# Normalised rows of two layers moved from ScalarE to VectorE, and the expert slots, routing and softplus steps of a two-layer kernel put in another order

## The reference

```python
# layer 0, mixer: 16 heads of 64
Q = x @ W_Q + b_Q; K = x @ W_K + b_K; V = x @ W_V + b_V
x = x + softmax(Q K^T / 8) V @ W_O + b_O            # x on the right is layernorm(x)
# layer 0, feed-forward: top-1 of 8 experts, 512 hidden
gates = softmax((x @ wg_red.T) @ unit(wg).T); e = argmax(gates)
x = x + max(gates) * (gelu(x @ w1[e] + b1[e]) @ w2[e] + b2[e])
# layer 1, mixer: a Mamba block, 256 channels, 16 states
h = x @ fc1.T + b;  xc, z = split(h @ in_proj.T)
u = silu(causal_conv4(xc) + conv_b);  dt_low, Bm, Cm = split(u @ x_proj.T)
dt = softplus(dt_low @ dt_proj.T + dt_b)
state = exp(dt * A) * state + (dt * u) * Bm;  y = sum(state * Cm) + u * D
x = x + (y * silu(z)) @ out_proj.T @ fc2.T + fc2_b
# layer 1, feed-forward: every one of 8 experts (256 hidden), summed, times a gate close to 1
```

## Time and profile before

| | us |
|---|---|
| median of 3 runs | 1217.61 |
| the profiled execution | 1217.61 |
| its span, first to last instruction | 1216.3 |
| PE busy | 1128.7 (93%) |
| DVE busy | 832.1 (68%) |
| POOL busy | 781.9 (64%) |
| ACT busy | 583.4 (48%) |

### The profile page before, as it was taken

The page is one execution under the profiler, slowest core; times in us unless marked ns, Lnnn a source line. Parts: engine busy times, 40 slices in busy tenths (PEclk is TensorE's granted clock), DMA queues, the critical chain, the costliest instruction groups (busy, mean ns, idle before and its releaser), DMA issues.

```text
span 1216.3 us, 19302 instructions
## 1 busy us (share of the span) xinstructions
PE 1128.7 (93%) x7541; PEld 660.3 (54%) x7541; DVE 832.1 (68%) x1248; ACT 583.4 (48%) x805; POOL 781.9 (64%) x410
## 2 busy tenths in 40 slices
PE   5899999999999999999999999968788988779998
PEld 2455555555555555555655556956434434335786
DVE  5565567566566566556575556535889889998887
ACT  3434444443443444443434444537864576443654
POOL 4577778677777777767579882272586678883100
PEclk9899999999999999999999999989898989999999
DMA  6000000000000000000000115364463344440000
GB/s 195 2 1 1 1 1 1 2 1 1 2 2 1 2 1 1 2 2 1 1 2 14 51 48 195 100 199 187 157 216 132 118 136 138 147 147 18 9 9 18
DMA packets 38058, 68.83 MB, mean 57 GB/s; under 512 B 5936, under 2 KB 24112, under 8 KB 37968
## 3 DMA queue, kind: packets, MB, share of 16 engines
q1 hardware_dynamic: 32624, 47.75, 12.3%
q0 software_dynamic: 5344, 19.86, 4.7%
HBM read 61.30 MB, written 6.16 MB: 55 GB/s over the span
## 4 chain that ended last, share of the span: by engine, by line
PE 77%; DVE 8%; issue 6%; POOL 6%; ACT 3%; DMA 1%; POOLq 0%; SPq 0%; DVEq 0%; ACTq 0%
PE psum L564 19%; PE psum L533 16%; PE psum L550 6%; PE psum L580 5%; PE psum L537 5%; POOL hc L1937 4%; PE psum L642 3%; PE psum L926 3%; PE psum L845 3%; PE psum L909 3%; PE psum L595 2%; PE psum L615 2%; DVE psum L1632 2%; PE psum L708 2%; DVE hs L1639 2%
## 5 line engine op out<-in xcount | busy, mean ns | idle before, releaser
L1830 POOL TENSOR_TENSOR psums<-psums,prob 128x1024 f32<-128x1024 f32 x180 | 426.6, 2370 | 104.2 <-ACT prob L998 82.7
L1347 DVE TENSOR_REDUCE mx<-psum 128x2 f32<-128x1024 f32 x256 | 302.0, 1220 | 211.2 <-PE psum L550 211.2
L998 ACT ACTIVATE prob<-psum 128x1024 f32<-128x1024 f32 x256 | 243.1, 1025 | 218.2 <-PE psum L537 218.2
L564 PE MATMUL psum<-prob,V 128*64 128x512 f32 x1024 | 258.4, 604 | 0.0
L1937 POOL TENSOR_TENSOR hc<-hs,cc 128x1024 f32<-128x1024 f32 x64 | 151.3, 2364 | 73.9 <-DVE hs L1639 72.7
L1639 DVE TENSOR_TENSOR_SCAN hs<-dA,psum 128x1024 f32<-128x1024 f32 x64 | 146.3, 2287 | 2.7 <-DVE psum L1632 0.7
L845 PE MATMUL psum<-hc,ident 128*128 128x512 f32 x256 | 126.7, 619 | 3.0 <-POOL hc L1937 2.9
L564 PEld LDWEIGHTS psum<-prob,V 128*64 128x64 f32 x1024 | 62.0, 136 | 98.3 <-issue 92.6
L1830 POOL TENSOR_TENSOR psums<-prob 128x1024 f32<-128x1024 f32 x30 | 71.5, 2382 | 62.9 <-ACT prob L998 62.9
L533 PE MATMUL psum<-q_hi,k_hi 64*128 64x512 f32 x512 | 108.4, 419 | 0.0
L537 PE MATMUL psum<-guard,row_one 64*128 64x512 f32 x512 | 101.7, 393 | 2.2 <-DMA guard<-mrow 2.2
(11 more groups left out here) (255 smaller groups left out, 1702.6 us busy)
## 6 DMA issues: line engine op xcount, KB each, us to landing
cc<-C_rows SPq DMA_DIRECT2D x64, 512.0 KB, 3.7
slots_in<-e_zero SPq DMA_DIRECT2D x2, 960.0 KB, 8.2
slots_out<-e_y SPq DMA_DIRECT2D x30, 64.0 KB, 3.1
slot_rows_h<-slots_in SPq DMA_DIRECT2D x6, 256.0 KB, 3.0
x<-in_x SPq DMA_DIRECT2D x2, 512.0 KB, 5.1
e_w<-in_e_w SPq DMA_DIRECT2D x1, 1024.0 KB, 8.8
out_x<-x SPq DMA_DIRECT2D x4, 256.0 KB, 2.3
wk<-in_wk SPq DMA_DIRECT2D x1, 512.0 KB, 4.7
```

Source lines behind the costliest of these rows:

```text
L564: ins = pe.matmul(A.O[HALF[s], :], A.V[pair % 2][:, j, s * DH:(s + 1) * DH], A.prob[unit(pair, c, j) % NPB][:, s * CH:(s + 1) * CH], start ...
L998: act.activation(A.prob[n % NPB][:, :], slots.bank("score", pair, c, j).rearrange("p s n -> p (s n)"), ACT.Exp, scale=float(DH) ** -0.5).t ...
L1347: dve.tensor_reduce(K.A.mx[:, :, t, c], slots.bank("max", pair, t, c), AXX, ALU.max).then_inc(*slots.inc("max", pair, t, c))
L1830: pool.tensor_tensor(total[:, :], (K.A.prob[(n - 1) % NPB] if j == 1 else total)[:, :], K.A.prob[n % NPB][:, :], ALU.add).then_inc(*K.psum ...
```

## The change

No arithmetic changes. `ACT_ROWS` loses 1 and 2, so the rows of the norms in pair 3 and pair 9 are normalised on DVE, and POOL no longer forms `shift` for them. In the expert slots of batch 0, `total` and `count` stand one to two slots later, and batch 1's first three weight fetches no longer stand ahead of the scatters. Batch 1's first slots stand later: before, three `up` and two `down` come ahead of the norm of the Mamba block, now two `up` and one `down`. In the first inputs the slots are interleaved with the taps in another way, the last two `up` and `gelu` stand ahead of `xpj`, and `xpj` waits for both halves of `u`. In the recurrence `yrow` of slots s+11 to s+14 stand one unit earlier, `back` and `rescale` too, `readd` of the second half one later, and the softplus steps of batch 1 are drawn together.

```diff
-ACT_ROWS, XDR_UNIT = (1, 2, 5, 6), 26
+ACT_ROWS, XDR_UNIT = (5, 6), 26
...
-                        6: [("logits", 1), ("choose", 1)], 7: [("total", 1), ("count", 1, 0), ("count", 1, 1)] + [("fetch", NSLOT + i) for i in range(3)],
-                        8: [("count", 1, 2)] + [("scatter", 1, q) for q in range(4)]}
+                        6: [("logits", 1), ("choose", 1)], 8: [("total", 1), ("count", 1, 0)], 9: [("count", 1, 1)],
+                        10: [("count", 1, 2)] + [("scatter", 1, q) for q in range(4)]}
...
-        beside[t // 2 + 6] += [("back", 1, t)]
-        beside[t // 2 + 8 + t // 6] += [("rescale", t)]
+        beside[t // 2 + 5] += [("back", 1, t)]
+        beside[t // 2 + 7 + t // 6] += [("rescale", t)]
...
-           2: [("down", n), ("down", n + 1), ("up", n + 2), ("up", n + 3), ("rate", 1), ("du", 0, 1)],
-           3: [("yrow", n), ("yrow", n + 1), ("gelu", n + 2), ("gelu", n + 3)], 4: [("down", n + 2), ("down", n + 3)],
+           2: [("down", n), ("down", n + 1), ("yrow", n), ("yrow", n + 1), ("up", n + 2), ("up", n + 3), ("rate", 1), ("du", 0, 1)],
+           3: [("gelu", n + 2), ("gelu", n + 3)], 4: [("down", n + 2), ("down", n + 3), ("yrow", n + 2), ("yrow", n + 3), ("e1_load",)], 6: [("wturn",)],
...
-           27: [("dtp", 1, 0), ("dtp_out", 1, 0)], 28: [("softexp", 1, 0)], 29: [("softlog", 1, 0), ("dt", 1, 0)], 30: [("du", 1, 0)], 31: [("inp", 1, 2)], 32: [("inp_out", 1, 2)],
+           27: [("dtp", 1, 0), ("dtp_out", 1, 0), ("softexp", 1, 0), ("softlog", 1, 0)], 28: [("dt", 1, 0)], 29: [("du", 1, 0)], 31: [("inp", 1, 2)], 32: [("inp_out", 1, 2)],
...
-        for k in range(KI):
-            pe.wait_ge(X.u_done, k + 1)
-            for c in range(NC):
...
+        pe.wait_ge(X.u_done, KI)
```

More of the change, by code:

```diff
@@ L272, in routed_order @@
         order += beside.get(n, []) + [("loads", n - 2)] * (n < 12) + [("skip",)] * (n == NSLOT)
-    order += [("rows", 1, 0), ("rows", 1, 1)] + [("back", 0, t) for t in range(NT)] + [("fetch", s + 3), ("fetch", s + 4)]
+    order += [("rows", 1, 0), ("rows", 1, 1)] + [("back", 0, t) for t in range(NT)] + [("fetch", s), ("fetch", s + 1)]
     order += [("turn", 1, 0), ("turned", 1, 0), ("rows", 1, 2), ("turn", 1, 1), ("turned", 1, 1), ("rows", 1, 3)]
-    order += [("up", s), ("gelu", s), ("up", s + 1), ("gelu", s + 1), ("down", s), ("down", s + 1)]
@@ L276, in routed_order @@
-    order += [("turn", 1, 2), ("turned", 1, 2), ("turn", 1, 3), ("turned", 1, 3), ("up", s + 2), ("gelu", s + 2)]
-    order += [("return", 0, t) for t in range(NT)] + [("lnvar", 4), ("lnroot", 4)] + [("fetch", s + i) for i in range(5, 13)]
-    return order + [("yrow", s), ("yrow", s + 1), ("lnrows", 4)]
+    order += [("return", 0, t) for t in range(NT)] + [("lnvar", 4), ("lnroot", 4)] + [("fetch", s + i) for i in range(2, 10)]
+    order += [("turn", 1, 2), ("turned", 1, 2), ("turn", 1, 3), ("turned", 1, 3), ("up", s), ("gelu", s), ("lnrows", 4)]
@@ L281, in first_inputs_order @@
+    return order + [("up", s + 1), ("gelu", s + 1), ("down", s), ("yrow", s)]
 def first_inputs_order():
     s = NSLOT
[L285 to L293, removed]
+    order = turned(4) + [("up", s + 2), ("fc1", 0), ("fc1_out", 0), ("gelu", s + 2), ("down", s + 1)]
@@ new lines, in first_inputs_order @@
+    order += [("inp", 0, 0), ("inp_out", 0, 0), ("yrow", s + 1), ("up", s + 3), ("gelu", s + 3), ("inp", 0, 1), ("inp_out", 0, 1), ("down", s + 2)]
+    taps = [("conv", 0, k, w) for k in range(KI) for w in range(DCONV)]
+    order += [taps[0], ("yrow", s + 2), taps[1], *slot(s + 4), ("fetch", s + 10)]
+    for i in range(1, 4):
+        order += taps[2 * i:2 * i + 2] + slot(s + 4 + i) + [("fetch", s + 10 + i)]
+    order += [("fetch", s + 14), ("up", s + 8), ("gelu", s + 8), ("down", s + 7), ("yrow", s + 7), ("silu", 0, 0), ("silu", 0, 1)]
@@ L294, in first_inputs_order @@
+    order += [("up", s + 9), ("down", s + 8), ("yrow", s + 8), ("gelu", s + 9), ("up", s + 10), ("gelu", s + 10), ("xpj", 0), ("xpj_take", 0), ("pick",), ("xpj_out", 0), ("dtp", 0, 0), ("xdr", 0), ("dtp", 0, 1)]
+    order += [("down", s + 9), ("yrow", s + 9), ("dtp_out", 0, 0), ("dtp_max",), ("softexp", 0, 0), ("down", s + 10), ("yrow", s + 10)]
     return order + [("softlog", 0, 0), ("dtp_out", 0, 1), ("dt", 0, 0), ("du", 0, 0)]
@@ L781, in pe_xpj @@
     if b == 0:
-        for k in range(KI):
-            pe.wait_ge(X.u_done, k + 1)
-            for c in range(NC):
[L785 to L791, removed]
+        pe.wait_ge(X.u_done, KI)
     for c in range(NC):
-        pe.wait_ge(*work.empty("mix", KI - 1, c))
+        if b:
+            pe.wait_ge(*work.empty("mix", KI - 1, c))
         pe.wait_ge(*work.free("xpj", b, c))
```

7 lines of the change are left out of this document (3 added, 4 removed).

## The result

| | before | after |
|---|---|---|
| median of 4 runs, us | 1217.39 (1215.68 to 1217.79) | 1228.59 (1227.26 to 1232.72) |
| ratio | | 1.0100, 95% interval 1.0074 to 1.0128 |
| profiled execution, its span | 1217.61, 1216.3 | 1229.24, 1227.9 |

Slower by 11.2 us; the two profiled executions differ by 11.6. The forecast was 1234.0 with a range of 1219 to 1238: the direction is right, the measured time lies inside the range, and the size is 5.4 us too high.

A forecast was written before the change was run, and what follows sets the result against it. PE was taken to bound attention, a chain of small steps and transfers 800 to 825 us, DVE the recurrence. 13.8 + 2.8 + 3.0 - 4.8 + 2.7 - 1.1 = +16.4 on 1217.6 gave 1234.0 us, range 1219 to 1238.

The forecast's parts named there:

- The norms: Attention, pairs 3 and 9: DVE's rows wait behind POOL's adds and make PE 6.9 us late in each pair, +13.8 us.
- each add (2.4 us) stands between two DVE rows: Norms in attention: POOL is let in after one DVE row, so DVE is done only at 212.9.
- rival 2: Norms: two rows pass between two adds, 2.6 us less per norm, +11.2 in all, 1228.8 us; chance 0.13.
- the forecast's 6.9: PE's lateness in us per norm pair, from waits for the `max` product's slot and then the output product's slot.
- Rival 1: Norms: the rows pass without waiting for further adds, only +2.6 is left, 1220.2 us; chance 0.26.
- Expert slots and the way to `fc1`: Scatters 0.8 us earlier, but `fc1` later behind slots waiting for weights; between +1.5 and +5.1, taken as +2.8 us.
- To the end of SiLU: First inputs: DVE stands 2.3 us before the second tap, and `gelu` of s+8 ahead of SiLU adds 0.7: +3.0 us.
- SiLU to unit 0: First inputs: Abs starts 5.1 us after SiLU instead of 10.0, first unit at 13.85 us instead of 18.7: -4.8 us.
- Recurrence: `yrow` ahead of units 3 and 5 costs +1.4 and +0.9, `readd` after unit 12 another 0.4: +2.7 us.
- Softplus of batch 1: Recurrence: unit 30's scan 2.2 us late, but `du` for unit 32 there 2.2 us earlier: -1.1 us.
- its 2.6 for the orders: All terms outside the norms, what is left if the rows pass: +2.6 us.

The follow-up runs named there:

- rows: The kernel before with only the norm rows of pairs 3 and 9 moved to DVE, every order as before: 1231.14 us, ratio 1.0104.
- split44: rows with four of the eight norm rows left in place and four moved behind the copy of `mrow`: 1239.17 us, ratio 1.0002.
- order: The changed kernel with the norm rows of pairs 3 and 9 back on ACT, so only the order changes: 1218.51 us, ratio 1.0001.
- tail: The kernel before with the last two `up` and `gelu` of batch 1 ahead of `xpj`: 1219.68 us, ratio 1.0001.
- swap: order with the second tap ahead of the `yrow` of s+2: 1244.75 us, one run.
- best: tail with the changed kernel's order of the recurrence: 1220.77 us, ratio 1.0008.
- tail2: tail with `up` and `gelu` of s+8, `down` and `yrow` of s+7 also ahead of the SiLU: 1235.35 us, ratio 0.9960.
- best2: tail2 with the changed kernel's order of the recurrence: 1236.42 us, ratio 0.9975.
- split56: rows with five norm rows first in pair 3 and six in pair 9, the rest later: 1243.73 us, one run.
- split77: rows with seven norm rows first in both pairs and one later: 1240.37 us, one run.

## Why the prediction was right, and where not

**The norms: mechanism right, size wrong (+13.8, measured +9.3).** DVE's rows stood behind POOL's adds in pairs 3 and 9, five passed first, and PE waited for the slot of the first `max` product. What failed is "each add (2.4 us) stands between two DVE rows". Two rows pass between adds: POOL's next add begins 0.15 us after the last has ended, and in that time the waiting row gets in and the next one right behind it. DVE was done at 211.2 - 1.7 = 209.5 instead of 212.9, with two adds in the way instead of three. The row on which 0.14 us of POOL's delay was read the earlier trace rows concerned DMA issues, not adds, and couldn't carry "one row, one add".

That is rival 2 (0.13), whose +4.3 a norm stands against 4.65 in each pair. The nearness is partly luck. Its 4.3 is all wait; the trace has 2.84 and 2.88 us of wait, and most of the other 1.8 is that PE's next steps ran at 1.2 GHz, a price that only the upper end of the forecast's range had. The wait for the output product, the last part of the forecast's 6.9, isn't there in after (in rows it is 0.37 us in pair 3 and 0.21 in pair 9). Rival 2's time, 1228.8, was met by luck too: the profile of after has 3.3 us in attention that no term had (the late start, the clock near 600 us), and the orders took back 1.3 where rival 2 had +2.6. Rival 1 ("the rows pass") is what split44 makes true, not the change.

The Trainium skill ("SBUF — State Buffer", "SBUF: two separate sides") has the lock held for a whole instruction by whoever comes first. The trace agrees, by the rows of 2.55 and 2.45 us that end as an add ends. What happens between two adds the rows show: two short DVE operations pass.

**Expert slots and the way to `fc1` (+2.8): +1.7.** The first scatter waits for `posi` (19.38 us of idle time on POOL), and is late by 11.84 where attention was late by 12.64: -0.8, as forecast. From there to `fc1` it is +2.5, by the waits forecast, for the weights of s+1, with the clock back at full from the `down` of s on. The prediction's 2.8 is `fc1` against before, with the 0.8 already in it, so it stands against +1.7 (+2.3 in order). The reference is itself a lucky one: rows and tail, whose orders here are those of before, have the first `inp` 1.6 and 1.8 us later than the profile of before, at the low clock. Against rows the changed order costs 0.2 us from the last pair to the first tap.

**To the end of SiLU (+3.0): +3.0, but not for the reason given.** The prediction added 2.3 us that DVE stands and 0.7 for the `gelu` of s+8. The stall of 2.07 us is there, and it costs nothing: the taps are done 0.94 us before the SiLU begins, and swap, without the stall, has the same distance from PE's `down` of s+2 to the SiLU as order. What sets the SiLU is the last `up` whose `gelu` stands ahead of it. In before that is the `up` of s+7, 12.06 us after `fc1`; after, it is that of s+8, 15.08 us after `fc1`, with four more halves of slots in front of it (3.6 us, less some 0.6 that PE lost before): +3.0. So the 0.7 had named the right step and was 2.3 too small, and the 2.3 for the stall made up for it. The number was right by luck.

**SiLU to unit 0 (-4.8): 13.9 us against 18.7, -4.8.** tail and tail2 show that it hangs on two moves together.

**Recurrence (+2.7): +0.05 up to unit 30 against the profile of before, but that is too kind.** The delays came as forecast or smaller (unit 4 +0.9, unit 5 +1.15, of which 0.4 went at unit 6), and units 12, 18 and 19 gave 2.7 back. Part of that is the change's: with `rescale` one unit earlier, `wback` waits 0.20 and 0.29 us for ACT's `zg` (after, order), where three profiles with the old order (before, tail, rows) have 2.37, 2.34 and 1.82. What came back at 18 and 19 isn't: rows and tail, with the old recurrence, gain 1.3 there on the profile of before as well. Between pairs of runs that differ in this order (best and tail, best2 and tail2, order and rows) the term is +2.8, +1.0 and +1.4. So +2.7 stands at the upper end of what the runs show, and one profile of before is no firm reference for a term of 2 us.

**Softplus of batch 1 (-1.1): -1.04** at unit 32; between the same three pairs of runs -0.2, -1.1 and -1.1 from unit 30 to 35.

**The sum.** The forecast had +16.4, the profiles differ by 11.6. The add too many took 4.5 off (2 x 2.25), the recurrence 2.65, `fc1` 1.1 and the softplus up to unit 35 0.2. Against that stand 3.3 in attention and 0.3 in the dense experts that no term had. So the step that made the forecast too high is the add too many. The timed runs, which don't rest on one profile of before, put +12.7 (10.8 to 14.4) on the rows and 0.1 (-1.5 to 1.7) on the orders: the forecast's 13.8 for the rows lies in that interval, although the step behind it is wrong, and its 2.6 for the orders doesn't.

## What to carry to other kernels

An operation that fits into an engine's idle time by its length can still hold that engine ten times as long (a row of 0.26 us stood for 2.5), if it reads and writes SBUF only, as these rows do, and the other of DVE and POOL has long operations pending: ask whether its last piece is through before the other engine asks, and count the long operations in the way, not the microseconds. A wait that is added in one place is paid only down to the next place where that engine stood anyway; follow it there before it enters the sum, as the DVE stall of 2.07 us shows, which the SiLU never saw. When one `gelu` is moved ahead on ACT, look at what PE's list has queued behind the step that waits for it; half the move gained nothing here (tail, first chip), both halves 0.4% (tail2, third chip).

## What was not expected of the hardware

- 0.03 us in POOL's arrival went with one add in the way or two, and so with 1.2 or 4.65 us on PE. The changed kernel's four runs span 5.5 us; whether this is why wasn't traced.
- Near 600 us the clock was at 1.2 GHz for a few us, with PE busy throughout by its rows. It cost 1.6 us in the profiles of after and of rows, behind the router's 128x8 products (L669 in after), and 3.2 in split56 and best2, behind the 128x1 products of a softmax's sums (L613 in best2). The first three had PE late in pair 9, but best2 has its norms on ACT as before and PE in time, and has the fall all the same; split77 had PE late and shows none. So the fall isn't tied to the rows on DVE. Why it comes isn't settled. best2:

```profile
600.00:606.00 6.00, 6.00 (x52) 4.97 (x52) 1.28 (x7) 0.00 (x0) 0.72 (x1) 0.67 0.01 3
```

- The same program took 1219, 1239 and 1241 us on three chips, with its attention of equal length; most of it lies in the stretch of expert slots and transfers behind it.
